# Flamingo-like stack, first attention: a tile's context transposed by DMA into its ring instead of by TensorE and ScalarE

## What is computed

```python
x = x + jnp.tanh(g_xattn[0]) * _L0_xattn_ref(_layernorm(x, axis=-1), ctx_768, Wq, Wk, Wv, Wo, bo)

# _L0_xattn_ref: 8 heads of 64, context of 96 columns, a sequence's 64 tokens see its own 64 context rows
q, k, v = x @ Wq, context @ Wk, context @ Wv        # split by heads
attn = softmax(einsum('bhsd,bhld->bhsl', q, k) * 64 ** -0.5)
out  = einsum('bhsl,bhld->bhsd', attn, v) @ Wo + bo
```

## Time and profile before

| what | value |
|---|---|
| median of 3 runs | 1878.68 us (1876.93 to 1880.79) |
| the profiled execution, its own time | 1875.75 us |
| its span, first to last instruction | 1873.8 us |
| mean granted TensorE clock over the span | 0.983 of full |
| instructions | 72646 |

### The profile page before, as it was taken

The page is one execution under the profiler, slowest core; times in us unless marked ns, Lnnn a source line. Parts: engine busy times, 40 slices in busy tenths (PEclk is TensorE's granted clock), DMA queues, the critical chain, the costliest instruction groups (busy, mean ns, idle before and its releaser), DMA issues. The chain is left out here.

```text
span 1873.8 us, 72646 instructions
## 1 busy us (share of the span) xinstructions
PE 1788.7 (95%) x28635; PEld 1313.7 (70%) x28635; DVE 1621.6 (87%) x3645; ACT 1548.9 (83%) x2773; POOL 662.9 (35%) x918
## 2 busy tenths in 40 slices
PE   6999998896999999999999999989999999999798
PEld 4787776542577777777777777767777777777587
DVE  5999998599799898989898988778999999988754
ACT  5999997475999999999999999867888888888543
POOL 3788887432000000000000000005666666655564
PEclk9999999898999999999999999999999999999899
DMA  7645444487000000000000001005665555533233
GB/s 178 138 95 100 97 95 89 152 317 262 15 13 15 13 15 13 13 13 12 16 10 18 11 15 51 2 15 126 162 160 150 155 145 154 147 72 70 68 116 121
DMA packets 312953, 160.66 MB, mean 86 GB/s; under 512 B 236558, under 2 KB 295862, under 8 KB 312374
## 3 DMA queue, kind: packets, MB, share of 16 engines
q1 hardware_dynamic: 312278, 157.95, 32.1%
q10 hardware_dynamic: 480, 0.05, 0.0%
HBM read 62.33 MB, written 36.83 MB: 53 GB/s over the span
## 5 line engine op out<-in xcount | busy, mean ns | idle before, releaser
L240 PEld LDWEIGHTS psE<-ew,h 128*128 128x128 f16 x6144 | 353.3, 98 | 33.8 <-DVE h L1803 5.0
L1803 DVE TENSOR_TENSOR h<-g,h 128x1024 f16<-128x1024 f32 x256 | 313.1, 1223 | 71.2 <-ACT h L1727 60.4
L240 PE MATMUL psE<-ew,h 128*128 128x128 f16 x6144 | 364.0, 219 | 2.6 <-DVE h L1803 2.6
L1722 ACT ACTIVATE g<-psH,eb1T 128x512 f32<-128x512 f32 x512 | 326.2, 679 | 19.5 <-PE psH L240 18.8
L815 POOL TENSOR_TENSOR Ph<-E,Ph 128x512 f16<-128x512 f32 x192 | 222.0, 1156 | 234.7 <-ACT Ph L769 234.7
L1876 POOL MEMSET rbias<- 64x384 f32 x1 | 0.4, 412 | 799.7 <-POOLq L133 799.7
L1727 ACT ACTIVATE h<-g 128x1024 f16<-128x1024 f32 x256 | 270.6, 1057 | 8.1
L721 ACT ACTIVATE vB<-psV 128x512 f16<-128x512 f32 x384 | 226.0, 589 | 50.4 <-PE psV L619 48.3
L842 DVE TENSOR_TENSOR vB<-psV,vB 128x512 f16<-128x512 f32 x384 | 248.3, 678 | 1.1 <-ACT vB L721 1.0
L619 PE MATMUL psV<-shared 96*64 96x512 f16 x1536 | 210.4, 380 | 1.5 <-DVE vB L842 1.5
L821 POOL TENSOR_TENSOR E<-E,rden 128x512 f32<-128x512 f32 x192 | 199.6, 1040 | 15.6 <-DVE rden L853 14.8
(11 more groups left out here) (313 smaller groups left out, 3387.9 us busy)
## 6 DMA issues: line engine op xcount, KB each, us to landing
keys_ahead<-shared SPq DMA_DIRECT2D x52, 512.0 KB, 4.9
shared<-keys_ahead SPq DMA_DIRECT2D x52, 512.0 KB, 3.6
rawe<-in_L_ffn_w_dram SPq DMA_DIRECT2D x32, 256.0 KB, 3.2
wb<-rw SPq DMA_DIRECT2D x64, 128.0 KB, 2.0
idx<-places SPq DMA_DIRECT2D x110, 64.0 KB, 2.6
out_dram<-x SPq DMA_DIRECT2D x7, 512.0 KB, 3.2
context_T<-shared SPq DMA_DIRECT2D x64, 48.0 KB, 2.4
PT<-Ph SPq DMA_TRANSPOSE x192, 2.8
```

The costliest lines, as they stand in the source:

```text
L240: last = e.matmul(to, a, b, start=start and n == 0, stop=stop and n == 2, **flags)
L1722: e.activation(g32[:, ft, :], psH[:, ft, :], ACT.Gelu_apprx_tanh, bias=b1T[:, a.expert(1) * FT + ft:a.expert(1) * FT + ft + 1]).then_inc(s ...
L1803: e.tensor_tensor(h[:, 1 - par, 1, 2 * q:2 * q + 2, :], g32[:, 2 * q:2 * q + 2, :], h[:, 1 - par, 0, 2 * q:2 * q + 2, :], ALU.subtract)\
```

## The change

The context's two halves of a tile, `cc[:, tp]`, 128 x 256 in fp16, are transposed by one DMA (`e.dma_start_transpose`) on SyncE's queue straight into the ring, all 128 rows of it (`cT0`; rows 96 to 127 come from the padding of `cc`). TensorE's four transposes and ScalarE's copy are gone, and with them the semaphores C and ct; the semaphores ctx0 to ctx3, one for each place of the ring, now say that a transposed context has landed. TensorE's keys and SyncE's store wait for them, and ScalarE waits for the one of unit j - 1 before it writes the high half of nx into the same place of `cc`. SyncE issues the DMA at the head of step j for nx, when the low half is there, the values that read the old content of the place are done and its store has landed; once before the loop for tile 0.

```diff
--- before.py
+++ after.py
@@ -157,6 +157,7 @@
     shared = sb(whole, "shared", [P, 2 * NE * 512], F16)
     AB1 = shared[0:DC, 0:64 * D].rearrange("p (w l g k) -> p w l g k", w=2, l=2, g=2)
     cT1 = shared[0:DC, 64 * D:64 * D + 8 * P].rearrange("p (r h t) -> p r h t", r=4, h=2)
+    cT0 = shared[:, 64 * D:64 * D + 8 * P].rearrange("p (r h t) -> p r h t", r=4, h=2)
     u1 = shared[:, 64 * D + 8 * P:64 * D + 8 * P + 6 * 8 * P].bitcast(F32).rearrange("p (s h l) -> p s h l", s=3, h=8)
     xna1 = shared[:, 120 * P:124 * P].bitcast(F32).rearrange("p (k d) -> p k d", k=2)
     lnt1 = shared[:, 124 * P:128 * P].bitcast(F32).rearrange("p (k t) -> p k t", k=4)
@@ -477,7 +478,6 @@
             psY = ps(c, "psY", [P, 512], F32)
             psXC = ps(c, "psXC", [P, 512], F32)
             psX = psXC[:, 0:P]
-            psC = psXC[:, P:2 * P].bitcast(F16).rearrange("p (k t) -> p k t", k=2)
 
             def half(hp):
                 return slice(64 * hp, 64 * hp + 64)
@@ -529,6 +529,8 @@
                 def _(e):
                     def body(j):
                         a, a2, nx = Unit(j, 0), Unit(j, 2), Unit(j, -1)
+                        if first and nx.on:
+                            transpose_context(e, nx)
                         if first and a.on and a.par == 0:
                             turn = a.j.mod(4)
                             if turn == 0 and a.j.off > 0:
@@ -550,7 +552,7 @@
                                 e.dma_start(ew.b1T[:, FT * n:FT * n + FT],
                                             I["L0_ffn_b1"][n].rearrange("(k p) -> p k", p=P)).then_inc(s["b1"], 16)
                         if a.opens and first:
-                            wait(e, s["ct"], a.t)
+                            wait(e, s[f"ctx{a.ring}"], ring(a.t, a.ring), 16)
                             e.dma_start(context_T[bass.ds(a.t.value, 1)].rearrange("o p k -> p (o k)"),
                                         cT[:, a.ring].rearrange("p h t -> p (h t)")).then_inc(s[f"stored{a.ring}"], 16)
                         elif a.opens:
@@ -570,6 +572,13 @@
                             if 18 <= j.off < 18 + 2 * NE1:
                                 rw.load_expert(e, (j.off - 18) // 2, j.off % 2)
 
+                    def transpose_context(e, a):
+                        wait(e, s["clo"], a.t)
+                        wait(e, s["Vb"], a.j - RING)
+                        wait(e, s[f"stored{a.ring}"], ring(a.t, a.ring) - 1, 16)
+                        e.dma_start_transpose(cT0[:, a.ring], cc[:, a.tp].rearrange("p h k -> p (h k)"))\
+                         .then_inc(s[f"ctx{a.ring}"], 16)
+
                     def load_context(e, a):
                         wait(e, s["Vb"], a.j - G * (RING - 1) - 1)
                         e.dma_start(cT[:, a.ring].rearrange("p h t -> p (h t)"),
@@ -591,6 +600,9 @@
                     if not first:
                         e.sem_inc(s["ctx0"], 16)
                         e.sem_inc(s["ul0"], 16)
+                    if first:
+                        e.wait_ge(s["cc_pad"], 1)
+                        transpose_context(e, Unit(Step(None, 0, -1), -1))
                     for j in range(U + 2):
                         body(Step(None, 0, j))
                         if routing and j == U - 4:
@@ -641,7 +653,7 @@
                         def tokens():
                             if nx.opens:
                                 wait(e, s["ln"], nx.t)
-                                wait(e, s["ct" if first else "xt"], nx.t - 1)
+                                wait(e, s["xt"], nx.t - 1)
                                 for m in range(2):
                                     last = e.matmul(psX[half(m)], xn[:, nx.tp, half(m)], ident32[:], start=True,
                                                     stop=True)
@@ -655,10 +667,7 @@
                             tokens()
                         if a.on:
                             if a.opens:
-                                if first:
-                                    wait(e, s["ct"], a.t)
-                                else:
-                                    wait(e, s[f"ctx{a.ring}"], ring(a.t, a.ring), 16)
+                                wait(e, s[f"ctx{a.ring}"], ring(a.t, a.ring), 16)
                             if not a.loaded:
                                 keys(a, 0)
                                 keys(a, 1)
@@ -680,11 +689,6 @@
                             values(a2, 0, "a", ready)
                         else:
                             ready()
-                        if first and nx.on:
-                            for hl in range(2):
-                                for m in range(2):
-                                    last = e.transpose(psC[half(m), hl, :], cc[:, nx.tp, hl, half(m)], ident16[:])
-                            last.then_inc(s["C"], 1)
                         if a.on:
                             if a.opens:
                                 wait(e, s["xt"], a.t)
@@ -699,7 +703,6 @@
                                                     u[:, a.slot, h:h + 4, half(b)], start=True, stop=True)
                             last.then_inc(s["S"], 1)
                     if first:
-                        e.wait_ge(s["cc_pad"], 1)
                         pipeline(e, body, -1, U + 4, 8, U - 1, 4)
                     else:
                         phases(e, body, U, 8, U)
@@ -730,7 +733,8 @@
                                 e.activation(xT[:, nx.tp, :], psX, ACT.Copy).then_inc(s["xt"], 1)
 
                         if first and nx.on:
-                            wait(e, s["C"], nx.t - 2)
+                            if a1.on:
+                                wait(e, s[f"ctx{a1.ring}"], ring(a1.t, a1.ring), 16)
                             e.activation(cc[:, nx.tp, 0, 0:DC], tile_of(nx.t, ctx32), ACT.Copy).then_inc(s["chi"], 1)
                         def normalised(nx):
                             wait(e, s["X"], nx.t - 2)
@@ -769,11 +773,6 @@
                             e.activation(Ph[:, a2.par, 0].rearrange("p k t -> p (k t)"),
                                          E[:, a2.four].rearrange("p h l -> p (h l)"), ACT.Copy)\
                              .then_inc(s["phi"], 1)
-                        if first and nx.on:
-                            wait(e, s["C"], nx.t)
-                            wait(e, s["Vb"], nx.j - RING)
-                            wait(e, s[f"stored{nx.ring}"], ring(nx.t, nx.ring) - 1, 16)
-                            e.activation(cT[:, nx.ring], psC[0:DC], ACT.Copy).then_inc(s["ct"], 1)
                     if first:
                         parts = (0, 8, 16, 32, 48, U)
                         for part, (lo, hi) in enumerate(zip(parts, parts[1:])):
```

## The result

The changed kernel takes 1885.0 us (median of 8 runs, 1883.63 to 1889.01), the one before 1878.57 (8 runs): a ratio of 1.0033, 95% interval 1.0024 to 1.0042, so 6.4 us slower. The forecast was 1881.6, in a range from 1874 to 1892. The profile of the kernel before is of an execution 2.8 us under its median, so the two profiled executions lie 13.3 us apart.

A forecast was written before the change was run, and what follows sets the result against it. First attention bound by TensorE in plain units, VectorE around normalisations. Start +6.9, filling units -0.7, transposes -6.8 + 2.0, crowded queue +1.5 = +2.9 us on 1878.68: 1881.6, range 1874 to 1892 (the forecast's own 1878.5 to 1885).

The forecast's parts named there:

- What bounds it, and the gain: First attention: TensorE freed of 0.12 us a unit over 57 units, 6.8 us, less 2.0 taken back around VectorE's normalisations.
- ScalarE's copy costs nothing: Steady loop: ScalarE does not set the pace, so its copy of the transposed context costs and gains nothing.
- The start, +6.9: Unit 0: first transpose waits behind SyncE's loads, issued 24.5, landing 28.7; first keys 6.9 us late, nothing hiding it.
- Rival A: The late start is absorbed by slack in the filling pipeline or a later wait for VectorE: 1874.7 us; chance 0.14.
- the 0.7 us that I took off for the filling units: First five units: the removed copy and transposes lie on the path, gaining 0.7 us (0 to 4.0).
- The room in a plain unit: SyncE's queue: transpose issue takes 0.6 us, landing 2.4; up to 3.0 us to landing costs nothing.
- Rival B: The DMA sets the pace, landing 4.1 us after issue: 1913 us, or 1893 at 3.4; chance 0.15.
- my slope of 0.05 us a unit for each 0.1 us: Steady loop: each 0.1 us of landing above 3.0 costs 0.05 a unit, 2.9 us in 57 units.
- The crowded steps, +1.5: Units 2 to 12, while x and context still load: late transposes cost 1.5 us for four units (0 to 4).
- The signs: Expected: first keys near 28.7, plain units 4.39, landings 2.2 to 2.7 us, no key waits after unit 12, more VectorE waits.
- rival C: Start and crowded units near their upper bounds, VectorE swallowing most of the gain: +7.7 us, 1886.4; chance 0.16.
- a gain of 44 us: TensorE's transposes priced by the Trainium skill's 390 ns each, not the profile row: 57 x 0.78 = 44 us, time 1837.

The follow-up runs named there:

- e4: The changed kernel with TensorE's four transposes of the context kept, into a bank nobody reads, no copy following: 1887.02 us, ratio 1.0042 to the kernel before.
- e11: The changed kernel with a 96x256 fp16 copy of constants on ScalarE where the copy of the transposed context stood: 1884.44 us.
- e5: The changed kernel with the first two transposes ahead of the loads, later x and context loads in quarters, gate query and temperature at step 50: 1876.03 us.
- e8: e5 with a second transpose of the same size, of constants, ahead of each tile's own from tile 4 on: 1925.38 us.
- e10: The changed kernel with four loads of two tiles a step in steps 2 to 9, the same bytes in 32 issues instead of 16: 1890.68 us.
- e7: The changed kernel with only the gate query's and the temperature's load moved from ahead of the loop to step 50: 1886.55 us.
- e1: The changed kernel with the transposes of tiles 0 and 1 issued ahead of the four loads: 1882.98 us.
- e6: The kernel before the change with the same late loads as e5: 1879.07 us, ratio 1.0002.
- e2: The changed kernel with the loads of tiles 48 to 63 moved from steps 6 to 9 to steps 12, 14, 16 and 18: 1883.35 us.

## Why the prediction was right, and where its terms were off

**What bounds it, and the gain: right in kind, too large.** The 0.12 us a unit is there within 0.01 (4.51 to 4.40; 0.11 in e4). Of 47 units from 13 to 60 that would be 5.6 us; the changed kernel makes up 2.9. VectorE takes the rest. I gave it 2.0 of 6.8; it took about 2.7 of 5.6. The waits of the weight loads for VectorE's low halves, 95 to 300 us, point to it: 7.6 us in 13 waits after, 3.4 in 10 before, and 4.2 in 11 with TensorE's transposes kept (e4). The rows are of the changed kernel, the one before and e4:

```profile
PEld psV L631 <- DVE vB L841: 7.6, 13, 1.9
PEld psV L619 <- DVE vB L842: 3.4, 10, 0.7
PEld psV L632 <- DVE vB L846: 4.2, 11, 0.7
```

**ScalarE's copy costs nothing: right**, by e11.

**The start, +6.9: right mechanism, size 5.0.** The transpose was issued at 24.26 as foreseen (24.5), but landed 2.6 us later, at 26.9, not 28.7; the store in the row had waited for more: ahead of it the gate query, issued at 20.34, took 7.6 us to land, here, issued at 19.74, 6.7. Rival A, that the delay is absorbed, falls: unit 0's 5.0 is 4.7 at unit 3 and 6.1 at unit 9, and where the cause is removed (e5) it is missing to the end. Of the 0.7 us that I took off for the filling units, 0.3 are there by unit 3.

**The room in a plain unit: right in latency, wrong in queue time.** I took 2.4 us to landing and 0.6 us of SyncE's queue. The first is 2.3. The second is 1.19, twice my value: I had put it between a store's and that of a transpose of 8 blocks, close to the store's, and with 2 blocks it takes as long as with 8. In plain units the queue still has a hole (117.72 + 0.57 to 119.54), so no harm came of it there; e8 and e10 show how near it is. Rival B, the DMA sets the pace in every unit, didn't happen, and my slope of 0.05 us a unit for each 0.1 us was never tested: e8 was meant to and hit the other bound.

**The crowded steps, +1.5: the term that was most too small.** From unit 3 to 13 the gap grew by 3.4 (e7), 3.8 (e1), 4.9 (e4), 5.2 (e11) and 7.5 us in the changed kernel's profile. Two things were missing in my 1.5. Some of the waits over 2 us are followed by several us at half the granted clock, and others are not (2.30 us in e4); this is the likely reason why the changed kernel's profile is the longest. And I had let the new transpose find the same landing times as before, though its own time in the queue pushes the loads and the large transposes behind it. e10 shows what such time costs; how much of the crowd's loss it is in the changed kernel was not tried apart.

**Not foreseen: the last units**, +1.0 from unit 60 to 63, with two more waits for the DMA (0.26 and 0.53 us) and landings of 3.3 and 3.9 us in place of 2.3. Every kernel with the new transpose shows it (+0.7 to +1.6), and e6, without it, +0.0. Why the landings are longer there was not tried.

**The signs.** As said, TensorE idled for the transposed context before the first keys, plain units took 4.40, the new transposes landed after 2.3 us (3.5 at most), and ScalarE waited longer for TensorE's token transposes, 33.7 us against 20.8 from 17 to 320 us. After unit 12 the keys did wait for the DMA, 0.41 us at 128.9 and twice at the end. And the waits for VectorE's low halves were not more than 10.2 us over the whole attention but 7.6: they grew from 95 us on, and are gone before, where the keys wait for the DMA instead.

**The sum.** 5.0 at the start, - 0.3 to unit 3, 3.4 to 5.2 in the crowd (the kernels other than the one of the long profile), - 2.9 in the plain units, + 1.0 at the end: + 6.2 to + 8.0, against + 6.4 measured and + 2.9 forecast. The measured 1885.0 lies in the range, and at the very edge of the forecast's own, 1878.5 to 1885. That it lies no farther out is in part luck: the start was put 1.9 us too high, and this hid as much of what the crowd, the gain and the last units fell short. It came out on the side of rival C, whose mechanism (start and crowd dear, VectorE swallows the gain) is the nearest to what happened, though its start was too large. One side sum was wrong: with a gain of 44 us in place of 6.8 the time would be 1844, not 1837, since the forecast from which the 44 were taken held the 6.8 already.

## What to carry to other kernels

A DMA that replaces on-chip work inherits everything ahead of it in its queue: add the bytes already in flight at each place where it is issued, the first tiles above all, before counting what the freed engine gains. Where they can be moved, as here, the same change went from 6.4 us slower to 2.2 faster without touching the change itself. And count the queue's own time by the issue, 1.2 us a transpose here for both sizes, against the pace of a unit.

## What the runs showed of the hardware

- A DMA transpose of 128x256 fp16 holds SyncE's queue as long as one of 128x1024: 1187 against 1233 ns, median. Its landing is shorter, 2.3 against 3.1 us.
- The issue that the profile shows as long (3.9 us for 8 KB) is only the next one behind a large load. Moved away, its time passed to the transposes after it.
- After an idle of 2.8 us TensorE's granted clock was 0.51 for 7 us, so that such a wait cost about double. An idle of 2.3 us in e4 left it at 1.00 over the next 7 us, as did the waits of up to 1.2 us in e2 from 50 to 95 us.
